# Value products of two cross attentions, regrouped into three groups per half sequence behind a ring of six turned tiles

## What is computed

```python
q = split_heads(norm(x) @ Wq)            # 16 heads of 16 channels
k = split_heads(ctx @ Wk)                # 1601 keys per sequence
v = split_heads(ctx @ Wv)
attn = softmax(q @ k.T (+ mask * -1e9))  # 64 queries x 1601 keys, per head
x = x + (attn @ v) @ Wo
```

## The kernel before, in words

| tile | k_unit | v_unit, even half | v_unit, odd half | scores | value products |
|---|---|---|---|---|---|
| 0 | | | | | tile 12 of the half before, ahead of the turn |
| 1 | yes | | | | |
| 2 | | | | chunk 1 of g+1 | 0, 1 |
| 3 | | yes | yes | | |
| 4 | yes | | | chunk 2 of g+1 | 2, 3 |
| 6 | | yes | yes | chunk 3 of g+1 | 4, 5 |
| 7 | yes | | | | |
| 8 | | | | | 6, 7 |
| 9 | | yes | | | |
| 10 | yes (66 columns) | | | sums of g-1 | 8, 9 |
| 11 | | yes | yes (one tile) | | |
| 12 | | | | chunk 0 of g+2 | 10, 11 |

## Time and profile before

### The profile page before, as it was taken

The page is one execution under the profiler, slowest core; times in us unless marked ns, Lnnn a source line. Parts: engine busy times, 40 slices in busy tenths (PEclk is TensorE's granted clock), DMA queues, the critical chain, the costliest instruction groups (busy, mean ns, idle before and its releaser), DMA issues. The chain is left out here.

```text
span 2204.3 us, 60066 instructions
## 1 busy us (share of the span) xinstructions
PE 2018.7 (92%) x25120; PEld 1572.2 (71%) x25120; DVE 1225.8 (56%) x3363; ACT 1189.6 (54%) x2297; POOL 466.2 (21%) x368
## 2 busy tenths in 40 slices
PE   6999999999999995588997999999999999997874
PEld 4777777777777772357995677777777777775553
DVE  4555555565555557935113356565555556565675
ACT  4555655665566554521322555666565556554671
POOL 3211212222221200211001233333222333300010
PEclk9999999999999997797998999999999999998767
DMA  3111111111111001003663212211121121100000
GB/s 123 42 32 32 32 32 41 38 43 36 32 32 32 7 2 58 0 10 115 210 230 112 57 47 57 56 47 47 48 72 47 51 54 55 35 2 23 1 1 26
DMA packets 68812, 111.08 MB, mean 50 GB/s; under 512 B 14520, under 2 KB 37312, under 8 KB 68544
## 3 DMA queue, kind: packets, MB, share of 16 engines
q1 hardware_dynamic: 68544, 107.23, 16.4%
HBM read 106.17 MB, written 1.05 MB: 49 GB/s over the span
## 5 line engine op out<-in xcount | busy, mean ns | idle before, releaser
L748 DVE CUSTOM_DVE_ANT_0 maps_d<-scores_d,mask_scaled_d 128x512 f32<-128x512 f32 (+1 forms) x512 | 263.6, 571 | 229.4 <-PE scores_d L531 229.4
L748 DVE CUSTOM_DVE_ANT_0 maps_a<-scores_a,no_mask_a 128x512 f32<-128x512 f32 (+1 forms) x512 | 263.6, 571 | 227.3 <-PE scores_a L531 227.3
L541 PE MATMUL turn_a<-const,maps_a 128*128 128x128 f32 (+1 forms) x1664 | 247.8, 279 | 0.2 <-ACT mapsT_a L666 0.2
L541 PE MATMUL turn_d<-const,maps_d 128*128 128x128 f32 (+1 forms) x1664 | 247.7, 279 | 0.2 <-ACT mapsT_d L666 0.2
L666 ACT ACTIVATE mapsT_d<-turn_d 128x512 f32<-128x512 f32 (+1 forms) x288 | 167.0, 593 | 147.1 <-PE turn_d L541 147.0
L666 ACT ACTIVATE mapsT_a<-turn_a 128x512 f32<-128x512 f32 (+1 forms) x288 | 167.0, 593 | 147.0 <-PE turn_a L541 146.9
L671 ACT ACTIVATE maps_a<-maps_a,neg_max_a 128x1024 f32<-128x1024 f32 (+1 forms) x256 | 222.5, 952 | 1.0 <-DVE neg_max_a L755 1.0
L671 ACT ACTIVATE maps_d<-maps_d,neg_max_d 128x1024 f32<-128x1024 f32 (+1 forms) x256 | 222.5, 952 | 1.0 <-DVE neg_max_d L755 1.0
L541 PEld LDWEIGHTS turn_d<-const,maps_d 128*128 128x128 f32 (+1 forms) x1664 | 184.7, 141 | 28.7 <-issue 0.8
L541 PEld LDWEIGHTS turn_a<-const,maps_a 128*128 128x128 f32 (+1 forms) x1664 | 184.6, 141 | 28.8 <-issue 0.8
L262 POOL CAST ctx_hi_a<-raw_a 128x1024 fp32r<-128x1024 f32 (+1 forms) x60 | 51.7, 862 | 524.2 <-issue 501.0
(11 more groups left out here) (408 smaller groups left out, 4382.7 us busy)
## 6 DMA issues: line engine op xcount, KB each, us to landing
w_c<-in_L_ffn_W SPq DMA_DIRECT2D x30, 1024.0 KB, 6.8
raw_a<-in_ctxT SPq DMA_DIRECT2D x48, 512.0 KB, 3.7
raw_d<-in_ctxT SPq DMA_DIRECT2D x48, 512.0 KB, 3.7
mask_scaled_d<-in_mask SPq DMA_DIRECT2D x32, 400.2 KB, 5.4
raw_a<-in_ctxT SPq DMA_DIRECT2D x16, 65.0 KB, 2.1
raw_d<-in_ctxT SPq DMA_DIRECT2D x16, 65.0 KB, 6.9
x<-in_x SPq DMA_DIRECT2D x1, 1024.0 KB, 5.6
Wk_c_b<-in_L_attn_Wk_c SPq DMA_DIRECT2D x1, 1024.0 KB
```

The lines of the kernel that those rows point to most:

```text
L541: ins = nc.tensor.transpose(TP[at % 2][0:r, P * j:P * j + P], maps[g % 2][:, j, P * t:P * t + r], chip.ident)
L748: nc.vector.tensor_tensor_reduce(maps[b][:, j, cols], SC[j][:, 0:w], mf[m % 2][:, cols] if masked else none[:, 0:w], 1.0, NEG, ALU.add, AL ...
```

## The change

The ring of turned tiles has six places instead of three, and the value products of a half sequence are made in three groups instead of six: tiles 0 to 3 behind tile 5, tiles 4 to 7 behind tile 9, and tiles 8 to 12 behind the turn of tile 0 of the next half sequence. That turn of tile 0 now stands ahead of the last group; before, tile 12's products stood ahead of it, directly behind those of tiles 10 and 11.

```diff
+VALUES_AT = {5: range(0, 4), 9: range(4, 8)}
+VALUES_BEHIND = range(8, KT)
...
-    RING = 3
+    RING = 6
...
             for g in range(GROUPS):
                 m, h = g // 2, g % 2
                 for t in range(KT):
+                    turn(g, t)
                     if t == 0 and g:
-                        values(g - 1, KT - 1)
-                    turn(g, t)
+                        for u in VALUES_BEHIND:
+                            values(g - 1, u)
...
-                    if t and t % 2 == 0:
-                        values(g, t - 2)
-                        values(g, t - 1)
-            values(GROUPS - 1, KT - 1)
+                    for u in VALUES_AT.get(t, ()):
+                        values(g, u)
+            for u in VALUES_BEHIND:
+                values(GROUPS - 1, u)
             spread_sums(GROUPS - 1)
             output(NT - 1)
```

## The result

The changed kernel takes 2250.82 us in the median of four runs (2249.34 to 2254.13), the kernel before 2205.6 us beside it. The ratio is 1.0203 with a 95% interval of 1.0191 to 1.0215: slower by 45 us. The prediction said 2243, between 2214 and 2255. Its median moves from 2205.6 to 2206.4 us between the series, so a difference between two changed kernels of different series can be off by about 1 us.

The account below looks back on a forecast made before the run. TensorE's queue was taken as the bound; +0.62 us per even and +0.53 per odd half, 30 each, gave 34.5 us, with the last sequences +35.5: 2243 us against the median, range 2214 to 2255.

Parts of the forecast that it names:

- What bounds the kernel, and the prices of a group: In both cross attentions TensorE's queue sets the time; a value tile costs 0.22 us, leaving a group 0.14, entering about 0.10.
- Scores to scores: Scores of tile 2 to tile 4: TensorE arrives at 3.50 us, waits 0.49 for VectorE's fourth instruction; change -0.10.
- the gain of a half without waits: By prices alone, three exits and about one entry less save some 0.42 us per half sequence.
- Scores of tile 6 to k_unit of tile 7: Without values 4 and 5, k_unit waits 0.45 us for ScalarE's copy of v_unit out of bank PJ; change -0.21.
- k_unit to k_unit, and k_unit to v_unit: Tile 7 to tile 10: +0.45 us even, +0.31 odd half; tile 10 to v_unit of tile 11: -0.46.
- The unshown price: The first product behind a turn takes about 0.09 us longer; a wait may remove this, taken as 0.05 per wait.
- v_unit of tile 11 to k_unit of tile 1: Up to the next half's k_unit: two more value tiles and turns 0 and 1 apart, +0.63 us.
- Faster: Rival, chance 0.08: the waits don't show because copies and maxima start earlier too; -35 us, 2172.
- Slower still: Rival, chance 0.05: ScalarE's exps end too late for its move of tile 11, so turn 0 waits; 2258 us.
- The ring: The ring of six costs nothing: a tile's place is freed at least five tiles ahead of its need.
- The last sequences: No projections there and waits exist already; only the last group is longer, by two tiles: +0.5 us a layer.
- all four waits: TensorE waits before scores of tile 4, k_unit of tile 7, and v_unit behind tiles 7 and 10: 0.49, 0.45, 0.25, 0.22 us.

## Why the prediction was right, step by step

*What bounds the kernel, and the prices of a group.* Right: the same four kinds of work on TensorE, with their order alone changed, cost 45 us. Exit and tile came out at the predicted numbers in groups of four and five.

*Scores to scores.* Right in its place and its size: a wait of 0.49 for VectorE's fourth instruction, shown by the run with short maxima. The 0.42 that the prediction reckons as the gain of a half without waits is not what it names as its parts: three exits of 0.14 and one entry of 0.10 are 0.52. The forecast doesn't rest on it; the two runs with all releasing work cut short put it near 0.48, by the argument given there.

*Scores of tile 6 to k_unit of tile 7.* The mechanism was right, shown by the short copy and by the pair put back; the term was mis-sized. I took ScalarE's release at some 0.07 (copy's end at 413.95, k_unit at 414.02), and it is 0.14 (425.10, 425.24). The interval changes by -0.14 for -0.21, and 60 x 0.07 = 4 us.

*k_unit to k_unit, and k_unit to v_unit.* The two waits for VectorE's copies are there, with v_unit at 1.31 for 1.30. A turn in front of the sums takes 0.49 behind values (430.42 to 430.91), where I had 0.43: +0.06 in an even half. In the odd half the same mistake stands as a wait "of some 0.14" in the two turns of 442.24: I set their 0.98 against 0.84 for turns in front of a projection. In front of the sums two turns take some 0.91, so the wait was about 0.07, and the odd half gains +0.39 instead of +0.31. Together 4.2 us. The wait in front of k_unit of tile 10 was misread too, without harm to the sum: it starts 0.60 behind the sums before and 0.37 behind them after, so the wait was 0.23 and not 0.17.

*The unshown price.* This is the largest miss. "When TensorE has stood waiting between them this may go": in four of the five places it does not. Behind its wait k_unit of tile 7 takes 1.24 from its first product to its last (425.24 to 426.48), as it took 1.25 without one, and the v_units of the even half keep their first distance of about 0.20. In the fifth place, v_unit of tile 11 in an odd half, most of it goes. These are its first two products before and after:

```profile
445.35 0.36 PE L108 MATMUL project_a<-wv_hi_a,ctx_hi_a 128*65 128x256 f32 x1
445.55 0.28 PE L109 MATMUL project_a<-wv_lo_a,ctx_hi_a 128*65 128x256 f32 x1
```
```profile
407.08 0.30 PE L108 MATMUL project_a<-wv_hi_a,ctx_hi_a 128*65 128x256 f32 x1
407.22 0.28 PE L109 MATMUL project_a<-wv_lo_a,ctx_hi_a 128*65 128x256 f32 x1
```

0.20 before and 0.14 after, in each of 14 odd halves; where the pair of tiles 8 and 9 covers the wait again, it is 0.20. That is most of why v_unit of tile 11 to k_unit of tile 1 grows by 0.53 and not 0.63 in an odd half. I took 0.05 per wait, 30 x 0.25 = 7.5 us in all; the rows give some 0.06 in one wait of five and 0.01 or less in the others, about 2 us. Without any of it the forecast was 43 us, 2 from the 45 measured. Why this one place differs is open.

*The rivals.* "Faster" supposed that the releasing engines would start earlier. They start at the same distance behind TensorE in both kernels: 0.32 for the copy of a v_unit or of the last 66 columns of keys, 0.43 or 0.44 for a copy of 512 columns of keys, and the fourth maximum 3.16 behind the scores after for 3.15 before. The rule of the Trainium skill that a change of tiling mode drains TensorE (TensorEngine Tiling (Array Packing), Key Properties), to which the prediction held this case nearest, has at most a small price here: about 0.1 us on each side of a group, and some 9 us for one turn put in the wrong place. That this price is a drain is not shown: a projection behind a turn has its second product some 0.08 late too, and both are marked 128*128, so no tiling mode changes between them. "Slower still", by ScalarE's exps, did not come up: no wait for it is in the list beyond the copy of v.

*The ring.* The ring costs nothing, as said, but the reason given is wrong: the place of tile 4 is freed behind tile 9 and needed by tile 10, so it is one tile ahead and not five. It holds nothing up, since TensorE makes those value products ahead of that turn in its own order.

*The last sequences.* +1 us expected; the last halves of both layers up to what follows give some -0.6, and the first ones a further -0.8. Why is open.

*In all.* The place of all four waits was right. The misses of size add up: some 5 us for the unshown price, 4 for ScalarE's release and 4 for the turn in front of the sums, less some 3 to 4 at the ends of the layers and in small rests, make the 45 measured of the 35.5 forecast.

## What to carry to other kernels

A busy share near 100% doesn't say how near the engine stands to waiting; measure from start to start, and write beside each wait on the engine's queue how long before the engine's arrival it is fulfilled. Small groups of independent work are cover: each costs its entry and exit (0.14 to 0.24 us here) and is worth the wait behind it, so drop those whose wait is shorter, and move other work, such as a small product that is due anyway, into the gap first. The deeper ring gave nothing by itself here; it gave the freedom to choose those places.

## What the runs showed of the hardware that was not expected

The first product behind a turn takes 0.08 us longer than the next even when TensorE has been idle for 0.34 us between them (0.31 from 425.24 to 425.55, where (426.48 - 425.55)/4 = 0.23 is the distance of the others). In one place, in the v_unit products marked 128*65, only some 0.03 of it is left behind a wait of about 0.2 us (0.14 for 0.12, with 0.20 where there is no wait). What this price is, no run here shows. And a wait of 0.2 or 0.3 us in front of a product may stand nowhere in the list of waits by releaser, only as an "issue" gap of the weight loads.
